# A decoder with two top-64 attention stages: each row of scores cut into 52 pieces in place of 64

## The reference

```python
scores = jnp.einsum('bhqd,bhkd->bhqk', qh, kh) / np.sqrt(DHEAD)
vals, idx = jax.lax.top_k(scores, topk)                       # topk = 64
scores = jnp.full_like(scores, neg).at[bI, hI, qI, idx].set(vals)
probs = jax.nn.softmax(scores, axis=-1)
ctx = jnp.einsum('bhqk,bhkd->bhqd', probs, vh)
```

## Time and profile before

| what | value |
|---|---|
| median of 3 runs | 9607.21 us (9586.43 to 9630.57) |
| the profiled execution, its own time | 9610.03 us |
| its span, first to last instruction | 9608.2 us |
| busy: PE, DVE, ACT, POOL | 74%, 72%, 46%, 41% of the span |
| mean granted clock of TensorE | 0.748 of full speed |
| maxima of the pieces (line 770) | 4 groups of 8192, 901 to 970 us busy each |
| instructions | 163672 |

### The profile page before, as it was taken

One profiled execution on the slowest core, in us unless ns is written; L12 is line 12 of the kernel. 1 busy time (PEld: TensorE's weight loads), 2 busy tenths in 40 slices (PEclk: granted clock), 3 DMA queues, 4 the chain that ended last, 5 costly groups with the idle time before them and its releaser, 6 DMA issues. The chain is left out here.

```text
span 9608.2 us, 163672 instructions
## 1 busy us (share of the span) xinstructions
PE 7068.8 (74%) x30924; PEld 2767.1 (29%) x30924; DVE 6895.6 (72%) x47725; ACT 4456.8 (46%) x8379; POOL 3936.4 (41%) x2613
## 2 busy tenths in 40 slices
PE   6888557666667656899766766656656789999983
PEld 2222222222222223555322222222223322222222
DVE  2655279999999997455399999999998343343423
ACT  1444246666666554111266767657656422222220
POOL 1000035555555443122155556545555045555550
PEclk7889656666666655799766677766766899999986
DMA  1000200000000000000100000000000311111103
GB/s 58 25 22 19 39 15 7 5 7 8 5 8 5 8 4 2 20 20 13 36 5 5 9 5 9 5 8 5 9 5 3 145 33 39 31 28 39 31 21 79
DMA packets 85686, 201.67 MB, mean 21 GB/s; under 512 B 25264, under 2 KB 39598, under 8 KB 80814
## 3 DMA queue, kind: packets, MB, share of 16 engines
q1 hardware_dynamic: 73390, 174.17, 6.6%
q10 hardware_dynamic: 11264, 16.79, 0.7%
HBM read 123.17 MB, written 66.95 MB: 20 GB/s over the span
## 5 line engine op out<-in xcount | busy, mean ns | idle before, releaser
L2100 DVE TENSOR_REDUCE l1xc_part_max<-l1xc_by_query 128x1 f32<-128x512 f32 (+1 forms) x1024 | 558.1, 571 | 875.6 <-PE l1xc_by_query L1959 856.1
L582 PE MATMUL l1ac_by_query<-l1ac_k_stack,l1ac_q_stack 97*128 (+1 forms) x1024 | 440.6, 496 | 831.4 <-ACT keep_xT L677 477.5
L770 DVE MAX8 l1ac_cand<-l1ac_score 128x8 f32<-128x32 f32 x8192 | 970.2, 192 | 27.9 <-ACT l1ac_score L677 16.7
L2058 ACT ACTIVATE l1xc_prob<-l1xc_less_max 128x512 f32<-128x512 f32 (+1 forms) x832 | 451.5, 594 | 1125.9 <-PE l1xc_less_max L1973 985.2
L770 DVE MAX8 l1ac_cand<-keep_xT 128x8 f32<-128x32 f32 x8192 | 962.6, 188 | 4.4
L582 PE MATMUL l0xc_by_query<-l0xc_k_stack,l0xc_q_stack 97*128 (+2 forms) x1024 | 385.8, 447 | 751.1 <-ACT keep_xT L677 492.4
L770 DVE MAX8 l0xc_cand<-l0xc_score 128x8 f32<-128x25 f32 (+1 forms) x8192 | 901.4, 180 | 27.4 <-ACT l0xc_score L677 15.8
L552 POOL TENSOR_SCALAR l1ac_lost<-l1ac_score,l1ac_tops 128x2048 bf16<-128x2048 f32 x128 | 696.0, 5437 | 512.5 <-DVE l1ac_tops L789 512.5
L770 DVE MAX8 l0xc_cand<-keep_xT 128x8 f32<-128x25 f32 (+1 forms) x8192 | 902.1, 180 | 4.4
L1921 POOL TENSOR_TENSOR l1xc_total<-l1xc_total,l1xc_prob 128x2048 f32<-128x2048 f32 (+1 forms) x176 | 794.0, 4511 | 72.2 <-POOL l1xc_v_tile L1931 71.9
L552 POOL TENSOR_SCALAR l1ac_lost<-keep_xT,l1ac_tops 128x2048 bf16<-128x2048 f32 x128 | 696.3, 5440 | 271.5 <-DVE l1ac_tops L789 271.5
(11 more groups left out here) (461 smaller groups left out, 14987.6 us busy)
## 6 DMA issues: line engine op xcount, KB each, us to landing
l1xc_k<-wide_k SPq DMA_DIRECT2D x32, 400.2 KB, 5.2
moe_w<-in_L_ffn_mlp_w_dram SPq DMA_DIRECT2D x16, 512.0 KB, 4.0
wide_q<-l1xp_full SPq DMA_DIRECT2D x8, 1024.0 KB, 3.9
wide_q_parts<-l1xp_parts SPq DMA_DIRECT2D x16, 512.0 KB, 5.6
l1xc_q_hm<-wide_q_parts SPq DMA_DIRECT2D x32, 256.0 KB, 3.8
l1xc_q<-wide_q SPq DMA_DIRECT2D x32, 256.0 KB, 5.7
wide_sums<-l1xc_o_out ACTq DMA_DIRECT2D x64, 128.0 KB, 2.3
l1xf_num<-wide_sums SPq DMA_DIRECT2D x16, 512.0 KB, 11.3
```

The costliest lines, as they stand in the source:

```text
L582: nc.tensor.matmul(sA[c % 2][:, 0:w], Qm[0:SHIFT_ROW, bass.ds(at + i * P, P)], Kb[0:SHIFT_ROW, bass.ds(at + a, w)], start=True, stop=True) ...
L770: seg = nc.vector.max(new[:, j:8 * NSEG:NSEG], score[i % 4][:, a:a + w])
L2058: nc.scalar.activation(prob[0:n, buf(j), c], yP[c % 2][0:n], ACT.Exp).then_inc(y_taken, 1)
L2100: nc.vector.tensor_reduce(part_max[:, i % 2, c:c + 1], a_bank(i, c)[:, 0:w], AX.X, ALU.max).then_inc(a_taken, 1)
```

## The change

NSEG goes from 64 to 52, and the borders of the pieces are rounded so that all are nearly as long: 30 or 31 elements for 1601 keys (before: 25, the last 26), 39 or 40 for 2048 (before: 32). `UPTO`, the width of `cand` and the number of pieces in a slice follow NSEG. The rest of the program stays: the instructions of PE, ACT, POOL and SP are the same and in the same order.

```diff
@@ attend_top
     key_chunks = tiles_of(nk, CH)
-    NSEG = 64
-    seg_w = nk // NSEG
-    segs = [(j * seg_w, seg_w if j < NSEG - 1 else nk - j * seg_w) for j in range(NSEG)]
+    NSEG = 52
+    edges = [(2 * j * nk + NSEG) // (2 * NSEG) for j in range(NSEG + 1)]
+    segs = [(edges[j], edges[j + 1] - edges[j]) for j in range(NSEG)]
     ROUNDS = TOPK // 8
     UPTO = [r * NSEG for r in (1, 1, 1, 2, 2, 3, 4, 8)]
```

## The result

| | before | after | ratio |
|---|---|---|---|
| first comparison, 4 runs each | 9610.42 us (9586.43 to 9630.57) | 9359.01 us (9328.49 to 9388.31) | 0.9739 [0.9700, 0.9778] |
| repeated with 9 and 5 runs | 9618.81 us | 9348.19 us | 0.9721 [0.9708, 0.9734] |

The change makes the kernel 2.6 to 2.8% faster. 9359 us lies in the range, 69 us above the forecast of 9290 us and 14 us above the forecast's own range. The profiled execution took 9361.8 us.

A forecast was written before the change was run, and what follows sets the result against it. DVE, busy 294 of 300 us and 297 of 300 inside the two top-64 stages, was taken to bound the kernel. 9608.2 - 369 - 231 + 244 + 26 + 10 = 9288, forecast 9290 us; own range 9240 to 9345, wider range 9188 to 9395.

The forecast's parts named there:

- The gain per tile: Top-64 stages on DVE: 12 fewer instructions save 0.72 us, narrower candidates 0.45 us, together 1.17 us a tile, 600 us.
- The fallbacks: Tiles searched anew on DVE: 11 in place of 4, the 7 new at 31.6 or 39.3 us each, +244 us.
- The late flag: ACT and PE deliver the slowest tile in four's flag before DVE's check; only four first-stage waits grow, +10 us.
- The check: DVE's flag load and branch, behind shorter covering work, cost 0.05 us a tile, +26 us.
- No cost for odd starts and for the chain's cover: DVE pieces starting at odd places, and three pieces between dependent chain steps, were both costed at nothing.
- ACT's wait for DVE: Sign in the new profile: ACT's wait for a score buffer falls by over half outside the fallbacks.
- (a): Both stages: ACT and PE partly become the pace, flag and check meet; 83 us more, 9373 us; chance 0.14.
- (b): DVE pieces: fixed cost exceeds what start distances show, another 0.2 us a tile saved; 9188 us; chance 0.07.
- the Trainium skill's 75 ns: Fixed cost per DVE instruction by the skill's section 5.2, against 60 ns from the trace; would give 9199 us.
- (c): Fallbacks on DVE outrun the gain: slower by over 0.5% from 18 new ones, 25 give 9933 us; chance 0.03.
- (d): No new fallback at all in the two stages: 9046 us; chance 0.02.
- (e): The DVE time saved in the stages turns wholly into waits, near 9600 us; chance 0.02.

The follow-up runs named there:

- n52_nocheck: Changed kernel (52 pieces) without the check's flag load, branch and fallback, the wait for the flag kept: 8906.4 us.
- n64_nocheck: Kernel before (64 pieces) without the check's flag load, branch and fallback, the wait for the flag kept: 9449.1 us.

## Why the prediction was right, and where it was short

Three pairs of runs, with 52 and with 64 pieces each, give the terms of the sum one by one (both stages, us):

| term | forecast | measured | from |
|---|---|---|---|
| fewer pieces, narrower candidates, later flag | -600 + 10 | -572 | n52_nocheck less n64_nocheck |
| load and branch of the check | +26 | +53, of them some 22 by late flags | 82.6 - 29.5 |
| 7 new fallbacks | +244 | +245 | 386.7 - 142.0 |
| both stages | -320 | -274 | and after |
| outside them | 0 | +26 | 4522.3 - 4496.1 |

- **What bounds the kernel** was right: the stages are DVE's, and what is taken from or put on it arrives in full.
- **The gain per tile**, 1.17 us, is 1.167 and 1.163 by the medians. The distances between starts gave both its parts.
- **The fallbacks** were right in number and price, for 52 and for 46 pieces. This term decided how much was left: with no fallback in either kernel the change is worth 5.2% (8988.8 against 9482.9 us).
- **The late flag is the term that was sized worst.** The place was right: the tile in four behind PE's combination of sums. It stood at +10 us and measured +40 (50.3 after less 10.2 before; 42.6 in the pair without fallback). The argument was that the flag comes out 8.0 us into the slowest tile, before the check, and that only the four waits of the earlier trace rows grow. They did, by 7.6 us, at the jumps of the loop; but in 42 more tiles of the first stage flag and check already meet, and the load starts about 0.5 us late. The bound of 1.3 us per four tiles (166 us for both stages) holds.
- **The check** was taken at 0.05 us a tile, +26 us, since most tiles show no idle at a cover only 0.1 us longer. The pairs give +53 with what the late flags do through load and branch, and some +31 without it. So the value for the cover alone was nearly right, partly by luck: the 48 idles of 0.17 us on which the argument leans are mostly the long branches, 43 of 256 tiles, and no sign that the cover was just short. The sign that was named, some 25 us of idle there, came out as 49, since it holds the late flags too.
- **No cost for odd starts and for the chain's cover**: nothing in the medians speaks against it. With the check out, 0.9 us of idle without releaser is left ahead of the replacements in the first stage and none in the second, so three pieces of 30 to 40 elements cover a chain step.
- **Outside the stages** nothing was changed, and the 26 us came from the spread of that part. Of the 72 us between the forecast and the profiled execution they are over a third; the 46 in the stages are late flags (some 30), the check itself (some 5) and a remainder that no row shows.
- **ACT's wait for DVE** was to fall by over half outside the fallbacks. In the second stage it did: 525.8 - 2 x 39.3 = 447 became 368.9 - 5 x 39.3 = 172. In the first, 455 became 449.6 - 5 x 31.6 = 292 (the sixth fallback, at 1329.7, lies before that window), so it fell by a third only. The search buffer is now also awaited from POOL in the second stage (90.1 us in 57 waits).
- **The rivals.** (a) gave nearly the right time, 9373 us, in part by luck. Its mechanism is there: flag and check meet in one tile of four. But it priced the stages the wrong way round, 19 us in the first and 64 in the second, where late flags grew by 27 and 13, and 26 us of the miss are chance outside the stages. That the flag is late because the transfers of the statistics rows lose their slack, as it says, no run tests. (b) fell, the pieces take 59 ns each and nothing more went with them; so did the Trainium skill's 75 ns (9199 us). (c), (d) and (e) fell with the count of 11 and with DVE at 97 and 98%.

## What to carry to other kernels

Where an engine is over 95% busy in a stage, distances between starts price a change of it to a few ns an instruction, and stage lengths between two fixed instructions show it to 2 us where the total wanders by 45 to 60. Work that depends on the data (here a search anew of a whole tile) belongs in the sum before anything else: it is counted on the host, and choosing a size by that count was worth 173 us here. The price of a branch is not the idle that the waits show: take it out of both kernels and compare. And idle for which the view names no releaser can still be a wait, here for a flag that is loaded ahead of a branch: compare the start of the load with the end of what makes the flag, tile by tile.

## What the runs showed of the hardware

- A load of a flag and a branch on DVE, placed behind one maximum and 3 or 4 pieces, cost 0.07 and 0.05 us a tile with 0.67 and 0.69 us of cover (16.8 and 12.7 us over 256 tiles), and 0.21 and 0.11 us with 0.56 and 0.58 us (54.5 and 28.1 us). The last two hold late flags.
- The branch lets go after 0.20 to 0.23 us, or after 0.49 to 0.57 us with the flag long there, and nothing lies between. Of 256 tiles 43 and 44 take the long way before, 57 and 58 after. After a turn of the loop, 48 tiles on, the same tile is long again (31 of 32 and 32 of 32 before, 37 of 40 and 43 of 43 after). So it goes with the place in the program and not with the data; what it is stays open.
- A load that waits for its flag starts 131 to 134 ns after the end of the instruction on ACT that writes it.
- At a jump of the loop over heads PE's branch (line 423) takes 3.3 to 4.9 us in the 52-piece kernel, 0.08 us where the loop ends. DVE, still in the turn before, waits up to 5.6 us for the flag that is made behind that jump, and then about 2.0 us at its own jump, ahead of its first piece.
- With the same matmuls, PE was busy for 1548.2 us of the first stage after and 1644.9 before, and the granted clock stood at 0.64 against 0.61 of full speed (0.72 against 0.69 in the second): the shorter stage went with a higher share of the 2.4 GHz level. It was not what made it shorter, since DVE sets the end.
